# Moving the first six heads' convolutions into six PSUM banks, and four other steps within their queues, in a long-convolution attention and mixture-of-experts kernel

## The chip, the cores and the metric

One core of a Trainium2 chip. The metric is the device time of one launch in microseconds, here the median of three runs. The profile is one further execution, taken by the hardware profiler. TensorE is called PE, VectorE DVE, ScalarE ACT, GpSimd POOL and SyncE SP below.

## The reference, cut to what matters

The inputs x and ctx are 8 x 256 x 512 (batch, rows, positions). Rows form 32 heads of 8. With y the causal convolution of a head's 64 products of context rows with that head's 512 taps, the first block is

```python
kv = einsum('bhil,bhjl->bijhl', k_, v_)              # k = v = ctx
y = irfft(rfft(kv, n=2 * L) * rfft(ssm_kernel, n=2 * L))[..., :L]
out = einsum('bijhl,bhil->bjhl', y + kv * D, q_)     # q = layernorm(x)
x = x + out
```

and the second adds to x a feed-forward block of its layer norm: 16 experts (top 4 of a softmax, capacity 256, width 352) and a shared one of width 704, silu(x @ gate) * (x @ up) @ down. All is float32.

## The kernel before, in words

**Tiling.** Four heads make a group g, so there are eight groups (NG = 8, GH = 4). A group has two tiles of 128 tokens. Positions lie on the partitions in four blocks (LB = 4). A convolution is a product with Toeplitz matrices made of the taps: block row lb takes lb + 1 products, 10 in all. The products of context rows (pairs, i <= j only, 288 columns) are the moving operand. For heads 0 to 3 taps and pairs go in unsplit (line 510, 20 matmul records: each such product shows as two). From head 4 on both are split into a high and a low part, and three products are summed (line 517, 30 matmuls). The results go to the four PSUM banks of yb; two banks gu serve the feed-forward block, two banks mb the transposes.

**A head.** POOL makes the pairs (pairs, line 1081); ACT rounds them (round_kv, L832); POOL makes the low part (low_kv, L1092); PE convolves (convolve, L487 on). DVE multiplies by q in fifteen instructions (multiply, L1286; L1299 and L1301), or in thirty by halves, for heads 0 to 3: banks 0 and 1 as soon as they are done, then banks 2 and 3. Then it adds up (add_up, L1315), which counts d_sum. PE may begin the next head's bank pair when the multiplication of it is through (d_half for the first pair, d_mul for both).

**A group.** Each engine has a function steps(g, ...), and all order is the order of its queue and the semaphore waits in it. In steps(1) of PE: head 4; mixed_out(0), eight transposes of the four heads' sums into mb, which waits for four sums; head 5; normalised(0), transposes of the normalised tokens; prep_ctx(2), transposes of group 2's context; gate_up(0, 0) and (0, 1), products of the tokens with the shared weights (L580); head 6; gate_up 2 and 3 with the router; prep_q(2); head 7; gate_up 4 and 5. On DVE: multiply head 4, add_x(0) (adds x, then the token statistics), add up head 4, low_tokens(0), and so on by heads with the middle steps between, and prep_stats (statistics of x for the next group, L1265 to L1271) in head 1 of a group. POOL's inverse_t and inverse_x follow the statistics, ACT's norm_tokens and norm_q follow these.

**Weight pieces.** The shared weights come in seven pieces: 0 to 3 of gate and up, 4 to 6 of down. SP loads a piece, ACT rounds it (split_shared, L786), POOL (pieces 0, 1, 3; L1103) or DVE (2, 4, 5, 6; L1248) makes the low part. Raw pieces share room, so SP loads piece 3 when 0 is through, 5 when 2 is, 6 when 4 is (load_split_slot). Piece 2 lies where x1, the sum of add_x, comes to lie.

**SP's queue** around the change, in order: group 0's tiles; taps of heads 0 and 1; tiles of group 1; piece 0; taps of heads 2 and 3; pieces 1 and 2; when piece 0 is through, piece 3; when head 2 is convolved, the taps of head 4; tiles of group 2; then as below (lines 407 to 421).

```python
            sp.wait_ge(conv, 4)
            load_toep(5, 1)
            load_shared(LB)

            sp.wait_ge(conv, 5)
            load_toep(6, 0)
            sp.wait_ge(sw_h, 3)
            low_done(sp, 2)
            load_shared(LB + 1)
            load_split_slot(LB + 2)
            sp.wait_ge(conv, 6)
            load_toep(7, 1)
```

## Time and profile before

| | |
|---|---|
| median of three runs | 641.11 us (640.76 to 641.79) |
| the profiled execution: time, span | 641.18 us, 639.4 us |
| mean granted PE clock | 0.984 |
| PE busy | 597.3 us, 93% |
| DVE busy | 475.8 us, 74% |
| POOL busy | 352.6 us, 55% |
| ACT busy | 278.7 us, 44% |

The span runs from the first to the last instruction; 1.8 us of the execution lie around it. Times in a timeline are microseconds from the span's start. The granted clock is a share of 2.4 GHz. "Idle before" is the time for which an engine had nothing to do just before an instruction, with what ended it. POOL's spans are rough. The convolutions of heads 0 to 7 and the feed-forward steps of group 0 fill the first 94 us; groups 1 to 7 follow, then the experts.

### The profile page before, as it was taken

The page shows a single profiled execution, that of the slowest core. Times are in us where ns is not written, and L with a number is a line of the kernel's source. Part 1 is how long each engine was busy: PE and PEld are TensorE (multiplying, and loading weights), DVE is VectorE, ACT ScalarE, POOL GpSimd, SP SyncE. Part 2 cuts the span into 40 slices and gives each one's busy share as a digit, 9 for nine tenths or more (in the row PEclk, how much of TensorE's full clock was granted, in tenths as well). Part 3 has the DMA queues.
Part 4 walks back from the last instruction along what each step waited for, and adds up shares of the span by engine and source line. Part 5 has one row for each costly group of instructions (what it writes and reads, how often), then busy time and mean ns, then how long its engine had stood idle before and what let it go on. Part 6 is the DMA issues. An engine that isn't in the chain of part 4 may idle for free.

```text
span 639.4 us, 13527 instructions
## 1 busy us (share of the span) xinstructions
PE 597.3 (93%) x4447; PEld 560.3 (88%) x4447; DVE 475.8 (74%) x1226; ACT 278.7 (44%) x499; POOL 352.6 (55%) x481
## 2 busy tenths in 40 slices
PE   4976999999999999999999989899999999999993
PEld 3666989999999999999999878889999999999992
DVE  4998877848768677777589868898878877888630
ACT  2341442423423423424342243466556656655731
POOL 6946787866857666676662363226534344333342
PEclk9987989999999999999999999999999999999997
DMA  7471513414225115222040051968888877888543
GB/s 191 160 210 67 197 34 100 132 37 142 89 67 164 54 53 156 66 82 82 33 118 17 26 176 38 322 172 263 231 258 226 227 208 229 233 237 238 152 55 44
DMA packets 49882, 89.27 MB, mean 140 GB/s; under 512 B 3924, under 2 KB 20308, under 8 KB 49832
## 3 DMA queue, kind: packets, MB, share of 16 engines
q1 hardware_dynamic: 42560, 71.77, 35.5%
q0 software_dynamic: 7168, 16.78, 12.5%
q8 instruction: 28, 0.46, 0.3%
q14 instruction: 22, 0.18, 0.1%
q10 hardware_dynamic: 104, 0.08, 0.1%
HBM read 71.66 MB, written 16.95 MB: 139 GB/s over the span
## 4 chain that ended last, share of the span: by engine, by line
PE 80%; DVE 9%; DMA 3%; issue 3%; POOL 2%; ACT 1%; DVEq 1%; POOLq 0%; ACTq 0%; SPq 0%
PE gu L580 17%; PE yb L517 16%; PE gu L716 13%; PE mb L731 10%; PE gu L610 7%; PE yb L716 7%; PE mb L484 3%; PE yb L510 2%; PE yb L484 2%; DVE prod L1299 1%; DVE prod L1301 1%; DMA raw_w<-in_L_ffn_w_up_dram 1%; PE yb L690 1%; DMA xg<-normalised_tokens,slot_rows 1%; DVE onehot L1542 1%
## 5 line engine op out<-in xcount | busy, mean ns | idle before, releaser
L580 PE MATMUL gu<-xT,sw 128*128 128x256 f32 (+2 forms) x1152 | 141.6, 281 | 0.0
L580 PEld LDWEIGHTS gu<-xT,sw 128*128 128x128 f32 (+2 forms) x1152 | 137.4, 180 | 0.3
L517 PE MATMUL yb<-kvh,toep 128*128 128x288 f32 x560 | 120.9, 304 | 6.0 <-DVE prod L1301 6.0
L1299 DVE TENSOR_TENSOR prod<-yb,qT 128x96 f32<-128x96 f32 (+11 forms) x288 | 78.5, 283 | 42.9 <-PE yb L517 37.6
L1092 POOL TENSOR_TENSOR kvl<-kv,kvh 128x1152 fp32r<-128x1152 f32 x28 | 75.2, 2686 | 55.9 <-ACT kvh L832 55.7
L1081 POOL TENSOR_TENSOR kv<-kT 128x256 f32 (+3 forms) x232 | 104.7, 492 | 0.0
L517 PEld LDWEIGHTS yb<-kvh,toep 128*128 128x128 f32 x560 | 94.7, 194 | 6.6 <-issue 6.6
L517 PE MATMUL yb<-kvl,toep 128*128 128x288 f32 x280 | 84.5, 302 | 0.0
L1315 DVE TENSOR_REDUCE oT<-prod 128x256 f32<-128x2048 f32 x32 | 72.9, 2278 | 0.1
L1301 DVE TENSOR_TENSOR prod<-yb,qT 128x96 f32<-128x96 f32 (+10 forms) x252 | 67.4, 267 | 0.0
L832 ACT ACTIVATE kvh<-kv 128x1152 fp32r<-128x1152 f32 x28 | 32.7, 1168 | 76.5 <-PE yb L517 42.4
L731 PE MATMUL mb<-ed,midh 128*128 128x512 f32 x180 | 57.5, 400 | 0.0
L1565 DVE TENSOR_TENSOR ew<-raw_w,ew 128x704 fp32r<-128x704 f32 x64 | 55.0, 882 | 0.8 <-ACT ew L952 0.8
L517 PEld LDWEIGHTS yb<-kvl,toep 128*128 128x128 f32 x280 | 54.6, 195 | 0.0
L1100 POOL TENSOR_TENSOR midl<-mid,midh 128x256 fp32r<-128x256 f32 x38 | 28.5, 758 | 41.1 <-ACT midh L848 41.1
L610 PE MATMUL gu<-sd,midh 128*128 128x512 f32 x160 | 49.8, 393 | 0.2 <-DVE midl L1359 0.2
L1200 POOL MEMSET carrier<- 128x1 f32 x16 | 2.1, 129 | 84.3 <-DVE slot_rows L1559 84.3
L716 PE MATMUL gu<-xgT,ew 128*128 128x256 f32 x384 | 47.2, 282 | 0.6 <-issue 0.6
L952 ACT ACTIVATE ew<-raw_w 128x704 fp32r<-128x704 f32 x64 | 45.4, 778 | 4.6 <-DMA raw_w<-in_L_ffn_w_up_dram 4.6
L716 PEld LDWEIGHTS gu<-xgT,ew 128*128 128x128 f32 x384 | 46.4, 189 | 0.9 <-issue 0.8
L716 PE MATMUL gu<-xT,ew 128*128 128x256 f32 x384 | 47.0, 282 | 0.0
L716 PEld LDWEIGHTS gu<-xT,ew 128*128 128x128 f32 x384 | 46.3, 190 | 0.2 <-issue 0.2
(182 smaller groups left out, 1073.0 us busy)
## 6 DMA issues: line engine op xcount, KB each, us to landing
toep<-toeplitz_taps SPq DMA_DIRECT2D x28, 512.0 KB, 3.6
raw_w<-in_L_ffn_w_gate_dram SPq DMA_DIRECT2D x16, 704.0 KB
raw_w<-in_L_ffn_w_up_dram SPq DMA_DIRECT2D x16, 704.0 KB
raw_d<-in_L_ffn_w_down_dram SPq DMA_DIRECT2D x16, 512.0 KB, 4.3
c_t<-in_ctx_dram SPq DMA_DIRECT2D x16, 256.0 KB, 4.5
x_t<-in_x_dram SPq DMA_DIRECT2D x16, 256.0 KB, 4.8
normalised_tokens<-xn SPq DMA_DIRECT2D x16, 256.0 KB, 2.9
out_dram<-yo SPq DMA_DIRECT2D x16, 256.0 KB, 3.0
```

What stands on the lines that cost most here:

```text
L517: last = pe.matmul(yb[:, lb, 0:PW], toep[s][:, a, d:d + P], rhs[:, s, m, :], start=(i == 0), stop=(i == len(steps) - 1))
L580: last = pe.matmul(gu[0:m, i % 2, u * GT:(u + 1) * GT], sw[:, c, a, col:col + m], xT[:, c, b, :], start=(c == 0 and (a, b) == PASSES[0]), ...
L610: last = pe.matmul(gu[:, t, :], (midh, midl)[a][:, j, cols], sd[:, j, b, :], start=False, stop=(j == SJ - 2 and (a, b) == PASSES[-1]))
L716: last = pe.matmul(egu[j][0:m, u * CAP:(u + 1) * CAP], ew[k][:, c, a, col:col + m], xgT[k][:, c, b, :], start=(c == 0 and (a, b) == PASSES ...
L731: last = pe.matmul(mb[:, h, :], lhs[0:EK[j], EJ * k + j, h * P:(h + 1) * P], ed[k][0:EK[j], j, b, :], start=(j == 0 and (a, b) == PASSES[0 ...
L952: act.activation(ew[k][:, c, 0, :], raw_w[k][:, c, :], ACT.Copy).then_inc(ew_h, 1)
L1081: last = pool.tensor_tensor(to[:, :, POFF[d]:POFF[d] + w], src[:, :, 0:w], src[:, :, d * B:HD * B], ALU.mult)
L1092: pool.tensor_tensor(kvl[:, s, :, :], kv[:, s, :, :], kvh[:, s, :, :].bitcast(fp32), ALU.subtract)\
L1299: last = dve.tensor_tensor(prod[:, s, lo:hi, d * B // 2:HD * B // 2, d, :], pair, first, ALU.mult)
L1301: last = dve.tensor_tensor(prod[:, s, lo:hi, 0:w // 2, HD - d, :], pair, second, ALU.mult)
L1315: dve.tensor_reduce(oT[:, :, hl * HD * B:(hl + 1) * HD * B].rearrange("p c (a u) -> p c a u", u=2), prod[:, s, :, :, :, :].rearrange("p c ...
L1565: dve.tensor_tensor(ew[k][:, c, 1, :], raw_w[k][:, c, :], ew[k][:, c, 0, :].bitcast(fp32), ALU.subtract).then_inc(ew_l, 1)
```

## The change

Heads 1, 2, 4 and 5 get other homes: half a head is a pair of banks, and the six banks of yb and gu are handed round among them; free() holds what each half has to wait for. Heads 4 and 5 are multiplied by halves, head 3 is not any more, and head 4's second half is multiplied first, after the whole convolution. mixed_out(0) and normalised(0) go between the halves of heads 4 and 5, on DVE add_x(0) goes ahead of head 4's multiplication and low_tokens(0) behind it. The statistics of x of group 1 go from head 1 of group 0 to ahead of head 0, their inverse on POOL ahead of head 5's pairs, and SP loads that x before the context. Weight piece 2 goes from DVE to POOL, ahead of piece 1. On DVE pieces 4 and 5 go one head later: 4 from behind head 4 to behind the x statistics in head 5, 5 from there to head 6. On ACT head 5's rounding and the evacuation of q go ahead of piece 3. SP's queue is otherwise as before.

```diff
--- before.py
+++ after.py
@@ -285,7 +285,7 @@
         carried = [sem("carried0"), sem("carried1")]
         N_CONST = 9
         SW_PIECES = LB + SJ // 2
-        POOL_PIECES = (0, 1, 3)
+        POOL_PIECES = (0, 2, 1, 3)
         DVE_PIECES = [p for p in range(SW_PIECES) if p not in POOL_PIECES]
 
         def low_done(eng, piece):
@@ -307,8 +307,16 @@
                 return kv[:, n, :, :]
             return kv_more[n - 2][:]
 
+        BY_HALVES = (0, 1, 2, GH, GH + 1)
+
         def by_halves(n):
-            return isinstance(n, int) and n < GH
+            return isinstance(n, int) and n in BY_HALVES
+
+        FIRST_HOMES = {1: ((gu, 0), (yb, 0)), 2: ((yb, 2), (gu, 0)), GH: ((gu, 0), (yb, 0)),
+                       GH + 1: ((yb, 2), (yb, 0))}
+
+        def home(n, half):
+            return FIRST_HOMES.get(n, ((yb, 0), (yb, 2)))[half] if isinstance(n, int) else ((yb, 0), (yb, 2))[half]
 
         ROUND = [slice(0, TT * (NG - 2)), slice(TT * (NG - 2), NT)]
 
@@ -387,9 +395,10 @@
             load_first(1)
             sp.wait_ge(taps_hl, 1)
             sp.dma_start(toep_dram, padhl[:].bitcast(fp32)).then_inc(taps_out, 16)
+            sp.wait_ge(x_stat, 1)
+            load_group(1, parts="x")
             sp.wait_ge(c_tr, TT)
-            sp.wait_ge(x_stat, 1)
-            load_group(1)
+            load_group(1, parts="c")
             load_shared(0)
             load_first(2)
             load_first(3)
@@ -484,6 +493,21 @@
                     last = pe.transpose(dst[:, c * P:(c + 1) * P], src(c), ident[:])
                 return last
 
+            def free(n, half):
+                if isinstance(n, int) and n < GH + 2:
+                    if n == 1 and half == 1:
+                        pe.wait_ge(d_half, 1)
+                    if n == 2:
+                        pe.wait_ge(*((d_mul, 1), (d_half, 2))[half])
+                    if n == 3:
+                        pe.wait_ge(*((d_mul, 2), (d_half, 3))[half])
+                    if n == GH:
+                        pe.wait_ge(d_mul, (3, 4)[half])
+                    if n == GH + 1:
+                        pe.wait_ge(*((d_mul, 4), (d_half, 4))[half])
+                elif half == 0:
+                    wait(pe, d_mul, n)
+
             def convolve(n, hl, between=None):
                 s = hl % 2
                 if whole(n):
@@ -497,24 +521,27 @@
                     pe.wait_ge(kv_l, n + 1 - GH)
                     pe.wait_ge(toep_in[s], 16 * ((n - GH - s) // 2 + 1) if isinstance(n, int)
                                else n * 8 - (8 * GH - 16 + 8 * s))
-                wait(pe, d_half if by_halves(n) else d_mul, n)
+                free(n, 0)
                 for lb in range(LB):
-                    if by_halves(n) and lb == LB // 2:
-                        last.then_inc(conv_half, 1)
+                    if lb == LB // 2:
+                        if by_halves(n):
+                            last.then_inc(conv_half, 1)
                         if between:
-                            between(0)
-                        wait(pe, d_mul, n)
+                            between()
+                        free(n, 1)
+                    bank, at = home(n, lb // 2)
+                    at += lb % 2
                     if whole(n):
                         for m in range(lb + 1):
                             d = (LB - 1 - lb + m) * P
-                            last = pe.matmul(yb[:, lb, 0:PW], toep[s][:, n // 2, d:d + P].bitcast(fp32),
+                            last = pe.matmul(bank[:, at, 0:PW], toep[s][:, n // 2, d:d + P].bitcast(fp32),
                                              whole_kv(n)[:, m, :], start=(m == 0), stop=(m == lb))
                         continue
                     steps = [(m, a, b) for m in range(lb + 1) for a, b in PASSES]
                     for i, (m, a, b) in enumerate(steps):
                         d = (LB - 1 - lb + m) * P
                         rhs = (kvh, kvl)[b]
-                        last = pe.matmul(yb[:, lb, 0:PW], toep[s][:, a, d:d + P], rhs[:, s, m, :],
+                        last = pe.matmul(bank[:, at, 0:PW], toep[s][:, a, d:d + P], rhs[:, s, m, :],
                                          start=(i == 0), stop=(i == len(steps) - 1))
                 last.then_inc(conv, 1)
 
@@ -562,8 +589,8 @@
                 j = ORDER[i]
                 if isinstance(g, int) and g == 0 and i == 0:
                     pe.wait_ge(sw_h, LB)
-                    low_done(pe, 2)
                     low_done(pe, 3)
+                    pe.wait_ge(d_mul, GH + 1)
                 pe.wait_ge(n_h, TT * g + TT)
                 pe.wait_ge(n_l, TT * g + TT)
                 if i < TT:
@@ -613,16 +640,15 @@
                         last.then_inc(dn_mm, 1)
 
             def steps(g, prep, post, chunk):
-                convolve(GH * g, 0)
-                if post:
+                if chunk:
+                    convolve(GH * g, 0)
                     mixed_out(g - 1, g)
-                if chunk:
                     down(g - 2)
-                if post and chunk:
                     normalised(g - 1)
-                convolve(GH * g + 1, 1)
-                if post and not chunk:
-                    normalised(g - 1)
+                    convolve(GH * g + 1, 1)
+                else:
+                    convolve(GH * g, 0, lambda: mixed_out(g - 1, g))
+                    convolve(GH * g + 1, 1, lambda: normalised(g - 1))
                 if prep:
                     prep_ctx(g + 1)
                 if post:
@@ -643,7 +669,7 @@
 
             pe.wait_ge(consts, 2)
             prep_ctx(0)
-            convolve(0, 0, prep_q)
+            convolve(0, 0, lambda: prep_q(0))
             prep_ctx(1)
             convolve(1, 1)
             pe.wait_ge(gate_in, 16)
@@ -931,9 +957,9 @@
             split_shared(2)
             norm_q(1)
             round_kv(GH, 0)
+            round_kv(GH + 1, 1)
+            evacuate(qT, 1, q_tr, q_ev, d_mul, 0)
             split_shared(3)
-            evacuate(qT, 1, q_tr, q_ev, d_mul, 0)
-            round_kv(GH + 1, 1)
             steps(1, True, True, (4, 5, None, 6))
             steps(2, True, True)
             with act.Fori(3, NG - 1) as g:
@@ -1147,10 +1173,11 @@
             pairs(2, 0, 2)
             pairs(3, 0, 3)
             pairs(GH, 1, 0)
+            inverse_x(1)
             pairs(GH + 1, 1, 1)
             split_shared(0)
-            inverse_x(1)
             low_kv(GH, 0)
+            split_shared(2)
             low_kv(GH + 1, 1)
             split_shared(1)
             steps(1, True, True, False)
@@ -1285,15 +1312,18 @@
 
             def multiply(n, g, hl):
                 s = hl % 2
-                dve.wait_ge(conv_half if by_halves(n) else conv, n + 1)
+                if by_halves(n) and n != GH:
+                    dve.wait_ge(conv_half, BY_HALVES.index(n) + 1)
+                else:
+                    dve.wait_ge(conv, n + 1)
                 dve.wait_ge(q_ev, TT * g + TT)
                 wait(dve, d_sum, n - 1)
                 q = qT[:, bass.ds(g % 2, 1), :, hl * HD * B:(hl + 1) * HD * B].rearrange("p s c w -> p (s c) w")
 
-                def blocks(lo, hi):
+                def blocks(lo, hi, bank=yb, at=0):
                     for d in range(HD):
                         w = (HD - d) * B
-                        pair = yb[:, lo:hi, POFF[d]:POFF[d] + w].rearrange("p c (a u) -> p c a u", u=2)
+                        pair = bank[:, at:at + hi - lo, POFF[d]:POFF[d] + w].rearrange("p c (a u) -> p c a u", u=2)
                         first = q[:, lo:hi, 0:w].rearrange("p c (a u) -> p c a u", u=2)
                         second = q[:, lo:hi, d * B:HD * B].rearrange("p c (a u) -> p c a u", u=2)
                         last = dve.tensor_tensor(prod[:, s, lo:hi, d * B // 2:HD * B // 2, d, :], pair, first, ALU.mult)
@@ -1301,10 +1331,13 @@
                             last = dve.tensor_tensor(prod[:, s, lo:hi, 0:w // 2, HD - d, :], pair, second, ALU.mult)
                     return last
 
-                if by_halves(n):
-                    blocks(0, LB // 2).then_inc(d_half, 1)
+                if by_halves(n) and n == GH:
+                    blocks(LB // 2, LB, *home(n, 1)).then_inc(d_half, 1)
+                    blocks(0, LB // 2, *home(n, 0)).then_inc(d_mul, 1)
+                elif by_halves(n):
+                    blocks(0, LB // 2, *home(n, 0)).then_inc(d_half, 1)
                     dve.wait_ge(conv, n + 1)
-                    blocks(LB // 2, LB).then_inc(d_mul, 1)
+                    blocks(LB // 2, LB, *home(n, 1)).then_inc(d_mul, 1)
                 else:
                     blocks(0, LB).then_inc(d_mul, 1)
 
@@ -1457,15 +1490,16 @@
                     add_x(g - 1)
                 if not prep:
                     start_round_one()
+                if post and not chunk:
+                    add_x(g - 1)
                 multiply(GH * g, g, 0)
                 if post and not chunk:
-                    add_x(g - 1)
+                    low_tokens(g - 1)
                 if chunk:
                     chunk_sum(g - 2, [0])
                 add_up(GH * g, g, 0)
                 if chunk:
                     chunk_sum(g - 2, [1])
-                if post:
                     low_tokens(g - 1)
                 for piece in extra[0:1]:
                     if piece:
@@ -1475,7 +1509,7 @@
                     if post:
                         middle(g - 1, 2 * hl - 2)
                     add_up(GH * g + hl, g, hl)
-                    if isinstance(g, int) and g == 0 and hl == 2:
+                    if isinstance(g, int) and g == 0 and hl == 1:
                         dve.wait_ge(gate_h, 1)
                         dve.tensor_tensor(sw[:, :, 1, IS:UP], mb[:, 0, 0:LB * E].rearrange("p (c e) -> p c e", c=LB),
                                           sw[:, :, 0, IS:UP].bitcast(fp32), ALU.subtract).then_inc(gate_l, 1)
@@ -1483,7 +1517,7 @@
                         low_rest(g - 1)
                     if post:
                         middle(g - 1, 2 * hl - 1)
-                    if prep and hl == 1:
+                    if prep and post and hl == 1:
                         prep_stats(g + 1)
                     for piece in extra[hl:hl + 1]:
                         if piece:
@@ -1521,9 +1555,9 @@
             link(dve.tensor_tensor(before_in_b[:], same_b[:], later_row[:], ALU.mult))
             dve.wait_ge(first_out, 16)
             dve.wait_ge(taps_out, 16)
+            prep_stats(1)
             steps(0, True, False, False)
-            split_shared(2)
-            steps(1, True, True, False, (4, 5, None, 6))
+            steps(1, True, True, False, (None, 4, 5, 6))
             steps(2, True, True, True)
             with dve.Fori(3, NG - 1) as g:
                 steps(g, True, True, True)
```

## Rows read from the trace of the kernel before

**Rows 1.** The page, busy time of each engine.

```profile
PE 597.3 (93%) x4447; PEld 560.3 (88%) x4447; DVE 475.8 (74%) x1226; ACT 278.7 (44%) x499; POOL 352.6 (55%) x481
```

**Rows 2.** Table of windows: busy us (x instructions) by engine, clock, DMA share, GB/s.

```profile
52.80:59.60 6.80, 6.80 (x31) 6.80 (x32) 5.07 (x10) 1.52 (x2) 3.56 (x4) 0.55 0.01 3
...
94.00:350.00 256.00, 256.00 (x1906) 246.53 (x1905) 190.14 (x547) 91.67 (x160) 168.94 (x250) 1.00 0.29 87
```

**Rows 3.** Timeline of PE: start, us, instruction, idle before.

```profile
43.42 0.37 PE L517 MATMUL yb<-kvh,toep 128*128 128x288 f32 x1 [1.44 <-DVE prod L1301]
...
52.80 0.58 PE L517 MATMUL yb<-kvh,toep 128*128 128x288 f32 x1 [4.31 <-DVE prod L1301]
...
63.05 5.87 PE L580 MATMUL gu<-xT,sw 128*80 128x256 f32 x48
...
82.43 0.37 PE L517 MATMUL yb<-kvh,toep 128*128 128x288 f32 x1 [0.25 <-DVE prod L1301]
...
88.01 5.80 PE L580 MATMUL gu<-xT,sw 128*128 128x256 f32 x48
```

**Rows 4.** Timeline of DVE, 16 to 80 us.

```profile
16.37 0.47 DVE L1299 TENSOR_TENSOR prod<-yb,qT 128x128 f32<-128x128 f32 x2 [3.16 <-ACT qT L824]
...
18.99 0.47 DVE L1299 TENSOR_TENSOR prod<-yb,qT 128x128 f32<-128x128 f32 x2 [0.49 <-PE yb L510]
...
29.75 0.14 DVE L1283 COPY carrier_d<-carrier_d 128x1 f32<-128x1 f32 x1
...
32.06 0.46 DVE L1299 TENSOR_TENSOR prod<-yb,qT 128x128 f32<-128x128 f32 x2
...
41.14 0.47 DVE L1299 TENSOR_TENSOR prod<-yb,qT 128x128 f32<-128x128 f32 x2 [0.44 <-PE yb L510]
...
45.51 4.04 DVE L1252 TENSOR_TENSOR sw<-x,sw 128x704 fp32r<-128x704 f32 x2
...
49.48 0.71 DVE L1299 TENSOR_TENSOR prod<-yb,qT 128x256 f32<-128x256 f32 x2
...
52.58 1.28 DVE L1325 TENSOR_TENSOR x<-mb,x_t 128x512 f32<-128x512 f32 x2
...
74.73 2.62 DVE L1270 TENSOR_SCALAR xnm<-xmv 128x2 f32<-128x2 f32 x1
...
77.33 1.84 DVE L1259 TENSOR_TENSOR sd<-x,sd 128x512 fp32r<-128x512 f32 x2
```

**Rows 5.** Timeline of SP's DMA queue.

```profile
9.80 1.20 SPq L330 DMA_DIRECT2D c_t<-in_ctx_dram  x2
...
33.03 0.39 SPq L340 DMA_DIRECT2D toep<-toeplitz_taps  x1
...
63.95 1.12 SPq L355 DMA_DIRECT2D yo<-in_L_ffn_sw_down_dram  x2
...
65.75 0.59 SPq L340 DMA_DIRECT2D toep<-toeplitz_taps  x1
```

**Rows 6.** DMA issues at 11, 33 and 65.8 us: size, us to landing.

```profile
x_t<-in_x_dram SPq DMA_DIRECT2D x2, 256.0 KB, 5.2
...
toep<-toeplitz_taps SPq DMA_DIRECT2D x1, 512.0 KB, 7.6
...
toep<-toeplitz_taps SPq DMA_DIRECT2D x1, 512.0 KB, 5.5
```

**Rows 7.** Timeline of POOL, 28 to 78 us.

```profile
28.73 3.33 POOL L1106 TENSOR_TENSOR sw<-sw_raw,sw 128x704 fp32r<-128x704 f32 x2
...
32.23 0.69 POOL L1059 TENSOR_TENSOR xrs<-xve,half_neg 128x2 f32<-128x2 f32 x1 [0.17 <-DVE xve L1271]
...
46.45 4.64 POOL L1106 TENSOR_TENSOR sw<-sw_raw,sw 128x704 fp32r<-128x704 f32 x2
...
74.66 2.67 POOL L1092 TENSOR_TENSOR kvl<-kv,kvh 128x1152 fp32r<-128x1152 f32 x1 [2.54 <-ACT kvh L832]
```

**Rows 8.** Timeline of ACT, group 0's first silu.

```profile
69.15 0.38 ACT L838 ACTIVATE sil<-gu 64x256 f32<-64x256 f32 x1
```

## The prediction

> **What bounds the kernel now.** I read the page first: TensorE (PE) is busy for 597.3 of 639.4 us [rows 1]. Next the table of windows: from 94 to 350 us PE has no idle time, at a full clock [rows 2], so the later stage neither waits for what is changed nor hides it. A microsecond by which PE reaches its work at 88 us earlier comes off the end. What matters lies before that, and PE's timeline gives the fixed points: head 4 begins at 43.42, head 5 at 52.80 behind 4.31 us of idle time, gate_up of group 0 at 63.05, head 7 at 82.43, and gate_up goes on at 88.01 [rows 3]. The waits ahead of heads 4, 5 and 7 were ended by VectorE (DVE), whose own timeline, read third, is nearly closed from 19 to 58 us. The windows show what an idle PE costs beside the gap: behind the 4.31 us the granted clock was 0.55 over 6.80 us, that is mostly the lower of its two levels, 1.2 GHz [rows 2]. The timeline of the DMA queue comes last; it decides here.
>
> I measure against the profiled execution, 641.18 us (span 639.4 and 1.8 around it); the median of the three runs is 641.11, the same thing. About 0.2%, 1.3 us, is what a measurement of this kernel can tell from no change.
>
> **Second x statistics.** They hold DVE from 29.75 to 32.06, 2.3 us in the middle of its closed stretch. Their new place is ahead of head 0's multiplication, where DVE is idle for 3.16 us before 16.37 [rows 4]. SP issues the two x tiles first, from 9.80, where the context tiles were [rows 5]; landing took 5.2 us [rows 6], so the second is there at 15.6, the statistics end near 17.5 and the multiplication starts 1.1 late. Of this 0.49 is taken up by the idle time before its second half at 18.99 [rows 4]. Net: about 1.8 us gained. The context tiles go out 1.2 later and land before 17; PE reads them behind head 0, after 18: nothing.
>
> **Heads 0 to 3 in six banks.** With heads 1 and 2 partly in gu, PE runs ahead of DVE and has head 3 done near 36, so DVE takes that in one piece. One piece costs 3.1 us (49.48 to 52.58); a half costs 2.1 (16.37 to 18.99 less the idle 0.49), two 4.2; and the 0.44 us of idle time inside head 3 goes [rows 4]: 1.6 us. Together the four sums, before at 45.51, are ready near 42. The gate's rounding, 0.2 us, only changes its place.
>
> **Weight piece 2.** It leaves DVE, where it stood between heads 3 and 4 for 4.04 us [rows 4], and comes to POOL, where such a piece takes 3.33 [rows 7]. POOL's queue is then: pairs of head 4, x inverse (0.69 us and a small product, 0.9), pairs of head 5, piece 0, low part of head 4, piece 2, low part of head 5, piece 1. With 2.67 for a low part it is empty near 45; with 4.64 for each of the last two pieces [rows 7] at 47.5; the token inverse behind it is wanted at 47.7. So: nothing, but with a cover of 0.2 to 3 us. The page GPSIMD Engine Reference of the Trainium skill (Engine selection) calls two-input elementwise work about twice as slow there and gives it to VectorE. The trace disagrees for this place: 3.33 us on POOL, 4.04 on DVE. By that rule POOL's piece would be 8 us and the inverse some 2 to 5 us late.
>
> **First mixed rows inside head 4.** SP's queue sets the date. POOL's piece 0 ends 0.9 later (the x inverse is ahead of it), so the taps of head 4, issued at 33.03 [rows 5] and landed 7.6 us later [rows 6], are there at 41.5. Before, PE wanted them at 43.42; now it has been idle since 37. Head 5, behind 4.31 us of idle time, took 6.7 us for 30 products, at about 0.24 each in its slow part [rows 2, 3]; I take the same for head 4. The first 9 products end at 43.7, the eight transposes at 45.1, the other 21 near 49. DVE's x addition, which now stands ahead of head 4's multiplication, starts at 44.4 where it had 52.58 [rows 4]; 3.2 us later its statistics are out, POOL's inverse ends at 48.6, ACT's first normalised tile at 49.4. Head 5's first half starts at 49.0 in its own banks, the transposes follow at 50.3, the second half ends at 54.1. DVE multiplies head 4 by halves, 49.0 to 53.1, and does the low tokens to 54.4. So the context transposes come then and gate_up begins at 55.3 instead of 63.05: **7.7 us** ahead. Its new wait for head 4's multiplication was met at 53.1.
>
> **Group 1 up to head 7.** DVE: sum of head 4 to 56.6, head 5 by halves to 60.7 (1.1 dearer than whole, but piece 4's 1.8 is gone from ahead of it). POOL: token inverse, piece 3, pairs of head 6 until near 55.6; ACT's first silu, bound to these, came at 69.15 [rows 8] and comes at 60.2. Both meet at 61, for DVE's first middle step. From there I keep the old spacing: the scalar step of the statistics, 74.73, comes at 65.8, **8.9 us** ahead. Then comes piece 4, where piece 5 was; that ended at 79.1 [rows 4], piece 4 ends at 70.2.
>
> **What is late next.** SP waits for piece 4's low part before it issues piece 6, and behind that in its queue stands the load of head 7's taps. Before, piece 4 was done ahead of head 5's multiplication: piece 6 was issued at 63.95, the taps at 65.75 [rows 5], 5.5 us to landing [rows 6], 11 us before head 7 wanted them. Piece 4 now stands behind head 5, two middle steps and the statistics. Done at 70.2, it lets the taps go at 72.1; they land at 77.6. DVE frees the yb banks 3.2 us after piece 4, at 73.4, and PE is ready then. Head 7 waits 4.1 us for its taps and begins at 77.6 instead of 82.43: only **4.8 us** ahead. PE stands still for over 4 us again, so I price head 7 like head 5, 6.7 us instead of 5.6 [rows 3], and gate_up follows at 84.3 instead of 88.01: **3.8 us**. Piece 6, the store and the next tiles shift with SP; head 8's taps go out near 76.5 and land by 84, before head 8 at 90. DVE's piece 5 fits ahead of head 7's end.
>
> **The sum.** gate_up gains 7.7; DVE adds 1.2; the taps take back 4.1; the clock 1.0: 3.8 us, all passed on by the closed PE stage. 641.2 less 3.8 is 637.4. Bounds: landings of 512 KB taps are 5.5 and 7.6 us [rows 6], so the stall can be 2 us longer (gain 1.7); head 4 at full clock would bring DVE's chain 1 us forward (gain 4.8).
>
> **Rivals.** (1) The taps stall, but less. The small scalar step in the x statistics took 2.62 us at 74.73 [rows 4], 0.07 us behind the start of POOL's 2.67 us low part at 74.66 [rows 7]. If POOL gets there a little later, that step is through first, and piece 4 and the taps come 2.4 us sooner; with head 4 at full clock too, 3.4. The gain is 6.2 to 7.2: 634 to 635. The page SBUF — State Buffer of the Trainium skill (Who interferes with whom) has a lock on a shared port pair, held by whoever issues first; the lengths, 2.62 beside 2.67, agree. For it: POOL has more work ahead. Against: both follow the same middle step, so the order may well repeat. Chance 0.22.
> (2) No stall: head 7 at 73.5, 8.7 us ahead, 632.5. It needs the taps within 1.3 us of issue, or another order in SP's queue, which the diff doesn't make. Chance 0.06, for an error in my reading of the queue.
> (3) About nothing: landings of 7.6 us, a slow clock for longer, and the cover at POOL's inverse gone by 1 us leave under 1.3. Chance 0.09.
> (4) **Slower,** by the same SP wait. Head 7 starts 7.4 us after piece 4 ends; it breaks even if piece 4 ends at 75.0 instead of 70.2, and each microsecond beyond costs one. It decides if POOL's token inverse is 7 us later than my sum, as with piece 2 at 8 us and its neighbours at 4.64. With 2 more the time is 643. No row here has a piece that long. Chance 0.04.
> The case of the sum has 0.59, its own range 635.4 to 639.4.
>
> **The numbers.** Faster by over 0.2%: 0.59, 0.22 and 0.06, 0.87. Same 0.09, slower 0.04. For eight in ten the range takes in rival (1) and the longer stall: 633.4 to 639.6.
>
> **What would show it.** The four sums near 42; the x addition near 44; gate_up at 55 to 56; the taps of head 7 issued 1.9 us behind DVE's piece 4; PE's wait before head 7 put down to that transfer, 3 to 6 us, with a low clock behind it; no new idle time of PE after 94. Wrong if head 7 starts as soon as head 6 is multiplied, if head 4 doesn't wait for its taps, or if POOL's inverse of tokens comes late.

## The result, and the profile after

The changed kernel takes 636.88 us (median of four runs, 634.94 to 637.20) beside 641.04 us before (four runs); the ratio is 0.9934, 95% interval 0.9923 to 0.9946. That is 4.2 us faster, forecast were 3.8 us and 637.4. The same kernel was run again later (636.51 us) and profiled a second time; where the two profiles of it differ, both are given below, since what differs between them can't be read as the effect of an edit.

The page of the changed kernel, its span and busy times, beside [rows 1]:

```profile
span 634.8 us, 13541 instructions
...
PE 596.0 (94%) x4447; PEld 559.9 (88%) x4447; DVE 474.2 (75%) x1239; ACT 278.9 (44%) x499; POOL 348.3 (55%) x483
```

PE does the same 4447 matmuls in almost the same busy time (596.0 us, before 597.3), in a span that is 4.6 us shorter: 3.3 us of what went is idle time, 1.3 us is busy time. The timeline of PE, for [rows 3]:

```profile
41.82 0.58 PE L544 MATMUL gu<-kvh,toep 128*128 128x288 f32 x1 [3.44 <-DMA toep<-toeplitz_taps]
...
44.12 1.50 PE L493 MATMUL mb<-ident,oT 128*128 128x128 f32 x8
...
55.32 5.83 PE L607 MATMUL gu<-xT,sw 128*80 128x256 f32 x48
...
77.95 0.58 PE L544 MATMUL yb<-kvh,toep 128*128 128x288 f32 x1 [3.93 <-DMA toep<-toeplitz_taps]
...
84.11 5.82 PE L607 MATMUL gu<-xT,sw 128*128 128x256 f32 x48
```

The mixed rows stand inside head 4, gate_up of group 0 begins at 55.32 instead of 63.05, 7.7 us ahead. Head 7 begins only 4.5 us ahead, at 77.95, and it is a transfer that it waited for, for 3.93 us. gate_up goes on at 84.11 instead of 88.01: 3.9 us. In the second profile of the same kernel everything here is 0.6 to 1.9 us earlier:

```profile
41.20 0.37 PE L544 MATMUL gu<-kvh,toep 128*128 128x288 f32 x1 [3.65 <-DMA toep<-toeplitz_taps]
...
76.61 0.58 PE L544 MATMUL yb<-kvh,toep 128*128 128x288 f32 x1 [3.64 <-DMA toep<-toeplitz_taps]
...
82.24 5.80 PE L607 MATMUL gu<-xT,sw 128*128 128x256 f32 x48
```

The two waits for taps are there in both, the rest of this section is the first profile. The table of windows, for [rows 2], shows (us, busy time and instructions of each engine, granted clock, DMA share, GB/s) the low clock behind each gap and the stage behind it:

```profile
41.00:44.00 3.00, 2.18 (x9) 2.21 (x10) 2.53 (x4) 0.00 (x0) 3.00 (x3) 0.61 1.05 253
...
46.00:50.00 4.00, 3.59 (x28) 3.35 (x26) 3.81 (x18) 1.48 (x3) 1.24 (x3) 1.00 0.20 57
...
78.00:84.00 6.00, 6.00 (x30) 6.00 (x31) 2.23 (x2) 0.40 (x1) 6.00 (x11) 0.61 0.91 270
...
94.00:350.00 256.00, 256.00 (x1907) 246.54 (x1905) 189.05 (x547) 91.38 (x159) 165.62 (x246) 1.00 0.29 87
```

The clock is 0.61 over 41 to 44 us, behind the gap before head 4, and 0.61 behind that before head 7; from 94 to 350 us PE is as closed as before. DVE's timeline, for [rows 4]:

```profile
15.00 0.15 DVE L1310 COPY carrier_d<-carrier_d 128x1 f32<-128x1 f32 x1 [1.77 <-DMA x_t<-in_x_dram]
...
20.78 0.47 DVE L1329 TENSOR_TENSOR prod<-yb,qT 128x128 f32<-128x128 f32 x2 [1.10 <-PE yb L537]
...
41.28 2.29 DVE L1348 TENSOR_REDUCE oT<-prod 128x256 f32<-128x2048 f32 x1
...
45.28 1.29 DVE L1358 TENSOR_TENSOR x<-mb,x_t 128x512 f32<-128x512 f32 x2 [1.72 <-PE mb L493]
...
66.58 2.62 DVE L1297 TENSOR_SCALAR xnm<-xmv 128x2 f32<-128x2 f32 x1
...
69.19 1.83 DVE L1286 TENSOR_TENSOR sd<-yo,sd 128x512 fp32r<-128x512 f32 x2
```

The statistics run in the idle stretch at 15.00, the last of the four sums is at 41.28 to 43.5, the x addition at 45.28 instead of 52.58. The scalar step still takes 2.62 us, and piece 4 comes behind it, at 69.19. The DMA queue, for [rows 5], then the landing of the taps of head 7, for [rows 6]:

```profile
34.60 0.39 SPq L348 DMA_DIRECT2D toep<-toeplitz_taps  x1
...
71.09 0.88 SPq L363 DMA_DIRECT2D yo<-in_L_ffn_sw_down_dram  x2
...
72.66 0.59 SPq L348 DMA_DIRECT2D toep<-toeplitz_taps  x1
```

```profile
toep<-toeplitz_taps SPq DMA_DIRECT2D x1, 512.0 KB, 5.0
```

DVE's piece 4 ends at 71.02, SP issues piece 6 at 71.09 and the taps at 72.66. They land 5.0 us later, at 77.7. Head 7 starts 0.3 us behind that. This is the chain that the prediction gave, from end to end.

### The profile page after: what moved, and what is told of

The parts are those of the page before. It is cut to its first block, busy times and chain, and to the rows that moved or that the text cites. A ratio compares the mean times of both kernels' runs of the same rounds, so it can differ in the third digit from the quotient of the medians.

```text
span 634.8 us, 13541 instructions
## 1 busy us (share of the span) xinstructions
PE 596.0 (94%) x4447; PEld 559.9 (88%) x4447; DVE 474.2 (75%) x1239; ACT 278.9 (44%) x499; POOL 348.3 (55%) x483
## 4 chain that ended last, share of the span: by engine, by line
PE 79%; POOL 6%; DVE 5%; DMA 4%; issue 3%; ACT 1%; SPq 0%; POOLq 0%; DVEq 0%; ACTq 0%
PE gu L607 17%; PE yb L544 16%; PE gu L742 13%; PE mb L757 10%; PE gu L637 8%; PE yb L742 7%; PE mb L493 3%; PE yb L493 2%; POOL kv L1107 2%; DMA toep<-toeplitz_taps 2%; DMA xg<-normalised_tokens,slot_rows 1%; POOL kv_more L1107 1%; POOL sw L1132 1%; PE yb L716 1%; DVE onehot L1576 1%
## 5 line engine op out<-in xcount | busy, mean ns | idle before, releaser
L544 PE MATMUL yb<-kvh,toep 128*128 128x288 f32 x554 | 117.8, 300 | 3.9 <-DMA toep<-toeplitz_taps 3.9
L1329 DVE TENSOR_TENSOR prod<-yb,qT 128x64 f32<-128x64 f32 (+10 forms) x272 | 74.6, 285 | 41.0 <-PE yb L544 38.7
L544 PEld LDWEIGHTS yb<-kvh,toep 128*128 128x128 f32 x554 | 92.1, 191 | 4.1 <-issue 4.1
L544 PE MATMUL yb<-kvl,toep 128*128 128x288 f32 x277 | 82.7, 299 | 0.0
L1331 DVE TENSOR_TENSOR prod<-yb,qT 128x96 f32<-128x96 f32 (+10 forms) x238 | 64.1, 269 | 0.0
L544 PEld LDWEIGHTS yb<-kvl,toep 128*128 128x128 f32 x277 | 53.1, 192 | 0.0
```

The costliest lines, as they stand in the source:

```text
L544: last = pe.matmul(bank[:, at, 0:PW], toep[s][:, a, d:d + P], rhs[:, s, m, :], start=(i == 0), stop=(i == len(steps) - 1))
L1329: last = dve.tensor_tensor(prod[:, s, lo:hi, d * B // 2:HD * B // 2, d, :], pair, first, ALU.mult)
L1331: last = dve.tensor_tensor(prod[:, s, lo:hi, 0:w // 2, HD - d, :], pair, second, ALU.mult)
```

## The experiments

Times are medians; each run is measured beside the kernel before on the same chip, and "beside before" is its median less that one's. "Second gate_up" is where gate_up goes on behind head 7 in the profiled execution, "rest" its span less that. The ratio with its interval is the recorded estimate and not always the quotient of the two medians: for the change, again, the medians differ by 4.2 us, the ratio 0.9948 makes it 3.3.

| run | us | before there | beside before | ratio, 95% interval | second gate_up | rest |
|---|---|---|---|---|---|---|
| the change | 636.88 | 641.04 | -4.2 | 0.9934, 0.9923 to 0.9946 | 84.11 | 550.7 |
| the change, again | 636.51 | 640.66 | -4.2 | 0.9948, 0.9932 to 0.9964 | 82.24 | 550.9 |
| taps of head 7 first | 632.75 | 640.73 | -8.0 | 0.9874, 0.9860 to 0.9888 | 78.44 | 552.8 |
| piece 4 early | 633.62 | 640.73 | -7.1 | 0.9887, 0.9873 to 0.9901 | 78.07 | 554.9 |
| before, taps of head 7 first | 640.77 | 640.73 | 0.0 | 0.9999, 0.9990 to 1.0008 | 87.85 | 551.3 |
| taps of head 4 first | 636.22 | 640.73 | -4.5 | 0.9931, 0.9919 to 0.9943 | 85.49 | 550.9 |
| x statistics back | 637.48 | 640.22 | -2.7 | 0.9958, 0.9944 to 0.9972 | 85.39 | 550.7 |
| piece 2 back | 636.11 | 640.22 | -4.1 | 0.9940, 0.9927 to 0.9954 | 82.07 | 550.9 |
| POOL later | 635.43 | 640.22 | -4.8 | 0.9925, 0.9911 to 0.9939 | 82.96 | 550.7 |
| PE kept busy | 635.57 | 640.22 | -4.7 | 0.9931, 0.9917 to 0.9944 | 82.23 | 550.9 |
| mixed rows back | 643.36 | 640.66 | +2.7 | 1.0040, 1.0024 to 1.0055 | 89.23 | 551.0 |
| banks back | 637.14 | 640.66 | -3.5 | 0.9953, 0.9940 to 0.9965 | 83.73 | 550.8 |
| combined | 635.12 | 640.66 | -5.5 | 0.9907, 0.9885 to 0.9929 | 80.76 | 552.0 |

The last column bears out the base of the sum: with the second gate_up anywhere between 82.07 and 89.23, what follows takes 550.7 to 551.0 us in the profiles of this kernel, so a microsecond won there is one won at the end. Only where it lies under 81 do some get lost again. One profile is not enough to read an edit worth under 2 us: in the two of the change the second gate_up stands at 84.11 and 82.24, and its ten executions lie between 634.93 and 639.27 us.

**Is it SP's queue that holds head 7?** One edit to the changed kernel, and the same edit to the kernel before:

```diff
-            load_split_slot(LB + 2)
             sp.wait_ge(conv, 6)
             load_toep(7, 1)
+            load_split_slot(LB + 2)
```

> The changed kernel, with SP issuing the taps of head 7 ahead of its wait for weight piece 4; nothing else. My theory (head 7 waits for its taps behind that wait, and the clock falls in the gap): taps issued near 55, head 7 starts at 74.2 as soon as head 6 is multiplied, instead of 77.95, takes 5.6 instead of 6.2 us; 4.3 us off the changed kernel, about 632.5. Rival, that the wait only happens to stand there and POOL's low part or the transposes of q hold head 7 anyway: no change, 636.9.

> The kernel before, with the same order in SP's queue as in the run with head 7's taps first. My theory: before, those taps landed 11 us early, so nothing moves, 641.0 within 0.6. Rival, that the order in SP's queue by itself gains (other transfers sooner): 638 or less.

Measured 632.75 and 640.77. SP's and PE's timelines of the changed kernel with the taps first:

```profile
54.82 0.38 SPq L348 DMA_DIRECT2D toep<-toeplitz_taps  x1
...
74.39 0.37 PE L544 MATMUL yb<-kvh,toep 128*128 128x288 f32 x1 [0.24 <-DVE prod L1331]
...
78.44 5.80 PE L607 MATMUL gu<-xT,sw 128*128 128x256 f32 x48
```

The taps go out at 54.82, head 7 starts at 74.39, released by DVE's multiplication of head 6, and takes 4.05 us with a granted clock of 1.00, less than the 5.6 that I had allowed. The stall is gone; in the kernel before the same edit moves nothing. So the change made this wait, and some 3.8 us of its gain went into it. The second gate_up comes 5.7 us ahead of the changed kernel's first profile, yet its span is only 3.6 us shorter (3.8 and 1.9 beside the second). PE's list of waits behind it has a new row:

```profile
PE gu L626 <- POOL midl L1126: 1.2, 1, 1.2
```

The down projection of group 0 waits for POOL's last low part, which ran from 89.28 to 90.54 beside DVE's piece 6 at 88.67. That is 1.2 of the 2.1 us by which the rest grew; the other 0.9 is not traced to one wait.

**Or piece 4's place?** The other way to free SP:

```diff
-            steps(1, True, True, False, (None, 4, 5, 6))
+            steps(1, True, True, False, (4, None, 5, 6))
```

> The changed kernel, with piece 4 on DVE put back behind head 4's sum, where it stood before; pieces 5 and 6 as in the change. My theory: SP is let go near 58, the stall is gone; DVE is idle for 1.27 us ahead of its first middle step at 61.4, so 1.8 us of piece cost only 0.6 there: head 7 at 74.8, 3.7 us off, about 633.2. Rival (DVE bounds group 1, piece 4 there costs its whole 1.8 us): 634.4. Rival (the wait is not the cause): 636.9 or more.

Measured 633.62. The taps of head 7 go out at 59.74. The piece takes 1.33 us of DVE at 56.76, and the first middle step comes 0.7 us later than in the changed kernel's first profile (62.09, there 61.42). This run has the earliest second gate_up, 78.07, and the longest rest, 554.9: behind the same wait of 1.2 us for POOL the clock was 0.72 over 90 to 96 us, with head 7's taps first it was 1.00:

```profile
90.00:96.00 6.00, 5.13 (x16) 4.09 (x17) 5.82 (x20) 1.86 (x3) 5.56 (x12) 0.72 0.13 42
...
90.00:96.00 6.00, 5.20 (x23) 4.36 (x24) 5.82 (x20) 1.92 (x3) 5.57 (x12) 1.00 0.15 55
```

Both ways agree: the cause is piece 4's new place together with the order behind it in SP's queue.

**The taps of head 4.**

```diff
-            sp.wait_ge(sw_h, 1)
-            low_done(sp, 0)
-            load_shared(3)
             sp.wait_ge(conv, 3)
             sp.wait_ge(taps_out, 16)
             load_toep(4, 0)
+            sp.wait_ge(sw_h, 1)
+            low_done(sp, 0)
+            load_shared(3)
```

> The changed kernel, with SP issuing the taps of head 4 ahead of piece 3 (behind head 2's convolution, near 32, instead of 34.60). My theory: they land near 37.5 instead of 41.8, head 4's first half runs at full clock near 38.4, the mixed rows wait for the four sums at 43.5 instead of 44.1, DVE's x addition starts about 0.9 earlier, head 7's taps too: 636.0. Rival: the gap moves behind the first half and the clock falls there all the same, no change, 636.9. Other rival (the stall at head 4 costs what PE stood still, 3.4 us): 633.5.

Measured 636.22. PE and DVE of this run:

```profile
42.77 1.09 PE L493 MATMUL mb<-ident,oT 128*128 128x128 f32 x8 [4.04 <-DVE oT L1348]
...
43.54 1.29 DVE L1358 TENSOR_TENSOR x<-mb,x_t 128x512 f32<-128x512 f32 x2 [0.82 <-PE mb L493]
...
70.98 0.59 SPq L348 DMA_DIRECT2D toep<-toeplitz_taps  x1
...
78.69 0.58 PE L544 MATMUL yb<-kvh,toep 128*128 128x288 f32 x1 [6.34 <-DMA toep<-toeplitz_taps]
```

The first half of head 4 no longer waits; the transposes wait 4.04 us for the four sums. The x addition starts at 43.54, 1.7 us ahead of the first profile of the change (45.28) but 0.5 ahead of the second (44.02), and the taps of head 7 go out 1.7 and 0.6 us sooner. In this execution they took 7.5 us to land instead of 5.0 and 4.8, and all was lost again. The median's gain of 0.3 beside the change is within the intervals, so my theory and the rival without a gain can't be told apart; 633.5, the rival that prices all that PE stood idle, is out. What stands: the wait at head 4 was worth 0.5 to 1.7 us of the 3.4 us at the x addition, and the landing of 512 KB scatters by more.

**The second x statistics, undone.** prep_stats(1) back into head 1 of DVE's queue, the context tiles first on SP, inverse_x(1) behind piece 0 on POOL.

```diff
-            prep_stats(1)
             steps(0, True, False, False)
...
-                    if prep and post and hl == 1:
+                    if prep and hl == 1:
...
-            inverse_x(1)
             pairs(GH + 1, 1, 1)
             split_shared(0)
+            inverse_x(1)
```

> The changed kernel, with the second x statistics undone: they stand again in head 1 of DVE's queue, SP loads the context tiles before x, POOL's x inverse is again behind piece 0. In the changed profile DVE is idle for 1.10 us in head 0 and 1.72 us before the x addition. My theory: the sums come 2.3 us later, 45.8, of which the wait of 1.7 us before the x addition covers a part: the taps of head 4 (0.9 us sooner again) no longer bind, and the addition is 1 to 1.5 us later: 638.0. Rival, worth its full 2.3 us: 639.2. Rival, hidden altogether: 636.9.

Measured 637.48, 2.7 us under the kernel before where the change is 4.2 under it: 1.4 us for this part by the medians, 1.5 or 0.6 by the ratios of the change's two sets, whose intervals this one's overlaps. The covered case is the nearest of the three, but nothing is clear of the noise. The x addition starts at 46.04, where the two profiles of the change have 45.28 and 44.02.

**Piece 2 back on DVE.**

```diff
-        POOL_PIECES = (0, 2, 1, 3)
+        POOL_PIECES = (0, 1, 3)
...
             steps(0, True, False, False)
+            split_shared(2)
             steps(1, True, True, False, (None, 4, 5, 6))
```

> The changed kernel, with piece 2 on DVE again, between head 3's sum and the x addition. DVE is idle there for 1.72 us in the changed profile. My theory: the piece runs beside POOL's piece 1 and takes about 4 us, 43.5 to 47.5, so the addition is 2.3 us later: 639.2. Rival (POOL, lighter by one piece, is done with piece 1 sooner, DVE's piece takes 2 us): no loss, 637.2.

Measured 636.11: nothing lost, the rival was right. DVE's piece, and POOL's last one before it:

```profile
42.34 1.68 DVE L1279 TENSOR_TENSOR sw<-x,sw 128x704 fp32r<-128x704 f32 x2
...
44.09 1.48 DVE L1358 TENSOR_TENSOR x<-mb,x_t 128x512 f32<-128x512 f32 x2
...
39.09 3.34 POOL L1133 TENSOR_TENSOR sw<-sw_raw,sw 128x704 fp32r<-128x704 f32 x2
```

POOL is through with piece 1 at 42.43, so the same two instructions that took 4.04 us before take 1.68 and fill the idle stretch ahead of the x addition at 44.09. The 4.04 us [rows 4] were DVE's piece beside POOL's low part and piece, not the price of the work. With the other engine out of the way such a piece takes 1.68 us on DVE; POOL's took 3.34. The medians show nothing that moving piece 2 to POOL earned once the rest was changed.

**Rival (1): the held scalar step.** One wait more on POOL:

```diff
                 pool.wait_ge(kv_m, n)
+                if isinstance(n, int) and n == GH + 3:
+                    pool.wait_ge(x_stat, 3)
```

> The changed kernel, with one wait added on POOL: the low part of head 7 begins only when DVE's x statistics of group 2 are through. Rival (1) of the prediction by itself. If the scalar step of 2.62 us at 66.58 is held by POOL's instruction: it takes 0.2, the statistics end 2.4 us sooner, piece 4 (then beside POOL's low part) ends 1 to 2.4 sooner and the taps with it: 634.6 to 636. If the 2.62 us are the step's own: no gain, 636.9 or up to 2 more, since POOL is late.

Measured 635.43. DVE and POOL of this run, where the changed kernel had 66.58 and 69.19:

```profile
66.67 0.17 DVE L1299 TENSOR_SCALAR xnm<-xmv 128x2 f32<-128x2 f32 x1
...
66.81 3.75 DVE L1288 TENSOR_TENSOR sd<-yo,sd 128x512 fp32r<-128x512 f32 x2
...
67.08 2.94 POOL L1120 TENSOR_TENSOR kvl<-kv,kvh 128x1152 fp32r<-128x1152 f32 x1 [3.03 <-DVE xve L1300]
```

The scalar step takes 0.17 us instead of 2.62. So the 2.6 us were a wait for POOL's instruction: the Trainium skill's page SBUF — State Buffer (Who interferes with whom) has this lock, and trace and page agree. But piece 4 then runs beside the low part and takes 3.75 us instead of 1.83; it ends at 70.56, in the profiles of the change at 71.02 and 69.95. Its end lies 0.54 us behind that of POOL's low part (67.08 and 2.94), as if its second instruction had waited for that one. The time is handed on, not won, and the rival's 2.4 us were wrongly priced. Beside the kernel before it stands 0.6 us better than the change, not more than the intervals allow.

**The clock behind the gap.** 28 products into a bank that head 7 overwrites, while PE waits for the taps:

```diff
+                    if isinstance(n, int) and n == GH + 3:
+                        pe.wait_ge(d_mul, n)
+                        for _ in range(28):
+                            pe.matmul(yb[:, 3, 0:GT], sw[:, 0, 0, 0:P], xT[:, 0, 0, :], start=True, stop=True)
                     pe.wait_ge(kv_h, n + 1 - GH)
```

> The changed kernel, with 28 further products of 256 columns on PE while it waits for head 7's taps, behind the multiplication of head 6, into a bank that head 7 overwrites; the computation is as before. They take 3.4 us at full clock and end near 77.6, ahead of the taps at 77.9. My theory (the low clock behind the gap costs what I summed): head 7 takes 4.1 to 4.3 instead of 6.2 us, gate_up starts at 82.1 instead of 84.1, 634.9. Rival (the clock falls all the same, as PE was idle at 71 to 73 too, and the added work is in the way): 637 to 639.

Measured 635.57. PE of this run:

```profile
73.64 3.62 PE L523 MATMUL yb<-xT,sw 128*128 128x256 f32 x28 [0.15 <-DVE prod L1335]
...
78.18 0.37 PE L548 MATMUL yb<-kvh,toep 128*128 128x288 f32 x1 [0.92 <-POOL kvl L1122]
...
82.23 5.80 PE L611 MATMUL gu<-xT,sw 128*128 128x256 f32 x48
```

The wait of 0.92 us is put down to POOL's low part, but head 7's was done at 68.64; it is the taps, issued at 72.13 and landed 5.8 us later, at 77.9. The granted clock is 1.00 throughout, from 72.4 to 82.23. Head 7 takes 4.05 us, as where its taps went first; in the two profiles of the change it took 6.16 (clock 0.62) and 5.63 (0.69). So the low clock cost 1.6 to 2.1 us there. The whole kernel doesn't show it: the second gate_up at 82.23 is 1.9 us ahead of the change's first profile and level with its second (82.24), where the taps had landed 1.5 us sooner. The median stands 4.7 us under the kernel before, the change's 4.2: no gain that can be told from none.

**The mixed rows, undone.** Banks, pieces and statistics as in the change, the old order on PE and DVE:

```diff
-                    convolve(GH * g, 0, lambda: mixed_out(g - 1, g))
-                    convolve(GH * g + 1, 1, lambda: normalised(g - 1))
+                    convolve(GH * g, 0)
+                    mixed_out(g - 1, g)
+                    convolve(GH * g + 1, 1)
+                    normalised(g - 1)
...
-                if post and not chunk:
-                    add_x(g - 1)
                 multiply(GH * g, g, 0)
                 if post and not chunk:
-                    low_tokens(g - 1)
+                    add_x(g - 1)
...
                 add_up(GH * g, g, 0)
+                if post and not chunk:
+                    low_tokens(g - 1)
```

> The changed kernel, with the mixed rows and the normalised tokens behind heads 4 and 5 again on PE, and on DVE the x addition behind head 4's multiplication; banks, statistics and pieces as in the change. My theory: the addition starts at 52 instead of 45.3, the whole chain to the normalised tokens is in a row again, gate_up begins near 60 instead of 55.3, piece 4 and the taps of head 7 are 3.5 to 5 us later: 640 to 641.5, so this part carries nearly the whole gain. Rival (the taps' stall absorbs it, as it hid DVE's work): under 638.

Measured 643.36, 2.7 us slower than the kernel before, 6.8 slower than the change and beyond the 641.5 that I had allowed.

```profile
51.35 1.28 DVE L1360 TENSOR_TENSOR x<-mb,x_t 128x512 f32<-128x512 f32 x2
...
56.93 1.97 PE L493 MATMUL mb<-ident,xn 128*128 128x128 f32 x8 [4.44 <-ACT xn L830]
...
61.95 6.43 PE L607 MATMUL gu<-xT,sw 128*80 128x256 f32 x48
...
83.64 0.56 PE L544 MATMUL yb<-kvh,toep 128*128 128x288 f32 x1 [3.30 <-DMA toep<-toeplitz_taps]
```

The x addition is at 51.35, PE is idle for 4.44 us before the normalised tokens and its clock is 0.50 behind it, gate_up begins at 61.95, near the old 63.05. With piece 4 still in its new place the stall at head 7 (3.30 us) comes on top. This part carries the whole gain: without it the other parts, with piece 4's late place among them, are a loss. What they would be with SP's order mended as well was not run.

**The banks of heads 0 to 3, undone.** The old homes and halves for these heads:

```diff
-        BY_HALVES = (0, 1, 2, GH, GH + 1)
+        BY_HALVES = (0, 1, 2, 3, GH, GH + 1)
...
-        FIRST_HOMES = {1: ((gu, 0), (yb, 0)), 2: ((yb, 2), (gu, 0)), GH: ((gu, 0), (yb, 0)),
+        FIRST_HOMES = {GH: ((gu, 0), (yb, 0)),
...
+                    if 1 <= n < GH:
+                        pe.wait_ge(*((d_half, n), (d_mul, n))[half])
```

> The changed kernel, with heads 0 to 3 in the four yb banks by halves as before (head 3 by halves too); heads 4 and 5 as in the change. My theory: DVE's sums come 1.6 us later (45.1), the transposes wait for them instead of for the taps of head 4, the x addition is at 46.3 instead of 45.3: 1 us slower than the changed kernel. Rival (the banks matter more, since PE gets behind DVE in heads 1 to 3): 2 us or more. Rival, nothing, since the taps of head 4 bind: 0.

Measured 637.14, 0.6 us over the change run beside it, within the intervals. From the start of the third sum to that of the fourth DVE takes 6.39 us in this run (35.14, 41.53) and 5.42 and 5.43 in the two profiles of the change: 1.0 us on DVE. The x addition, at 45.05, lies between those two (45.28 and 44.02), so neither the profiles nor the medians separate the 1 us of the first theory from none; 2 us is not seen.

**Combined.** The taps of heads 7 and 4 first, by the two edits of SP's queue above, and pieces 4 and 5 in their old places:

```diff
-            steps(1, True, True, False, (None, 4, 5, 6))
+            steps(1, True, True, False, (4, 5, None, 6))
```

> The changed kernel, with SP issuing the taps of head 7 ahead of its wait for piece 4, the taps of head 4 ahead of piece 3, and DVE's pieces 4 and 5 where they stood before (behind head 4 and behind the x statistics). Both stalls gone, and head 7's multiplication no longer behind piece 5, which held it by 2 us where only head 7's taps were moved. Expected: head 7 near 73.3, no new wait of PE at the down projection; 1.5 to 2.5 us under the run with head 7's taps first, 630.5 to 631.5. Rival (POOL's low parts bind by then): 632.7, as that run.

Measured 635.12 (631.20 to 636.11), 2.4 over the run with head 7's taps alone: my forecast was wrong, though one of the six executions took 631.20.

```profile
56.08 3.77 DVE L1286 TENSOR_TENSOR sd<-yo,sd 128x512 fp32r<-128x512 f32 x2
...
56.41 2.89 POOL L1118 TENSOR_TENSOR kvl<-kv,kvh 128x1152 fp32r<-128x1152 f32 x1 [1.28 <-ACT kvh L858]
...
64.07 0.37 PE L544 MATMUL yb<-kvh,toep 128*128 128x288 f32 x1 [3.31 <-DVE prod L1331]
```

Piece 4 begins at 56.08 and POOL's low part of head 6 at 56.41; side by side the piece takes 3.77 us. In the run with piece 4 early it began at 56.76, POOL's low part only at 58.22, and it took 1.33. DVE frees the banks that much later, and PE waits 3.31 us before head 6, in that run 0.73. That this is the whole loss was read from one profile; no run moved the low part to test it. The best kernel measured is the changed one with the taps of head 7 first, 632.75 us.

## Why the prediction was right

By its own steps, forecast beside the two profiles of the changed kernel:

| step | forecast | first | second |
|---|---|---|---|
| four sums ready | 42 | 43.5 | 42.7 |
| taps of head 4 landed, head 4 begins | 41.5 | 41.82 | 41.20 |
| x addition | 44.4 | 45.28 | 44.02 |
| gate_up | 55.3 | 55.32 | 54.48 |
| scalar step of the statistics | 65.8 | 66.58 | 65.52 |
| piece 4 done | 70.2 | 71.02 | 69.95 |
| taps of head 7 issued, landed | 72.1, 77.6 | 72.66, 77.7 | 71.59, 76.4 |
| head 7 begins | 77.6 | 77.95 | 76.61 |
| second gate_up | 84.3 | 84.11 | 82.24 |

Every step of the chain is there, in its order. That the median came within 0.5 us of the forecast is in part luck: single executions of this kernel spread over 4.3 us, and the second profile's gate_up is 2.1 us ahead of the forecast's.

**Second x statistics:** this term was too large. They start at 15.00 and head 0's multiplication 1.2 us late, as forecast (1.1), but the 0.49 us of idle time behind its first half didn't take it up: it grew to 1.10, since the first transposes on PE took 1.91 us and head 0's other half came at 16.60 where PE had 15.39 before. So head 0's sum starts 1.8 us later than before (22.94, before 21.15; 22.12 in the second profile) and not 0.6. The run with the statistics undone puts the worth of the part for the whole kernel at 0.6 to 1.5 us, within the noise; forecast 1.8 on DVE.

**Banks:** forecast 1.6 us on DVE. Beside the kernel before it is 1.6 (7.06 us from the third sum to the fourth, 5.42 after), beside the run without the part 1.0; at the end 0.6 by the medians, which can be none. PE's wait for the taps of head 4 can hide a part of DVE's gain, as the same sum had it.

**Piece 2:** the conclusion "nothing on POOL" holds (token inverse at 48.68, POOL idle for 3.26 us ahead of it). The gain of 4.04 us was mis-sized: the piece would have cost 1.68 us in the new order, in idle time. So was the comparison of 3.33 us on POOL with 4.04 on DVE, by which the prediction said that the trace disagreed with VectorE as the faster place: the 4.04 had been taken beside POOL's work, and with POOL idle it is 3.34 against 1.68, a factor of two. The total was not hurt, since the sum went by POOL's cover and the taps of head 4 and never by these 4 us alone.

**Mixed rows:** right in size (7.7 us at gate_up) and shown to carry the gain. Two errors cancelled in the first profile: the clock came back sooner than I took it (it was 0.96 over 45 to 46 us; the forecast's 49 for the end of head 4 puts it near 47), and the x addition was 0.9 us later.

**What is late next:** right, shown by undoing it from either end. **The clock:** 6.7 us forecast for head 7, 6.16 measured, so the term of 1.0 in the sum was 0.6, and nothing in the second profile, 5.63 (head 7 took 5.6 before, at a clock of 0.70). The whole price of the low clock there is larger, 1.6 to 2.1 us: it takes 4.05 with no gap ahead.

**Rivals:** (2) did not occur. Its 632.5 is what the kernel gives once the order in SP's queue is mended, 632.75. (1) fell: the lock is real, but its 2.4 us are handed to the next instruction; it was priced as if nothing stood behind the step. (3) fell with landings of 5.0 and 4.8 us. (4), slower, is not the change's case; taken without the mixed rows the other parts do come out slower than before, by 2.7 us, with the stall as one part.

Between the second gate_up (3.9 us) and the span (4.6 us) 0.7 us stay open: the rest is 551.4 us before and 550.7 after (550.9 in the change's second profile, 551.3 in the kernel before with head 7's taps first), and no experiment was made on it.

## What to carry to other kernels

When work is moved on one engine, look for queues on others that wait for it, and read what stands behind that wait: here a load with 11 us to spare became the bound because a piece of low parts ahead of it went one head later. A duration taken beside another engine's work isn't the price of an instruction (4.04 and 1.68 us for a piece of 128x704, 3.75, 1.83 and 1.33 for one of 128x512); before it is booked as a gain or moved, ask what runs beside it in the new place. And once one wait is gone, the gain holds only until the next engine is late: of 5.7 us at the second gate_up the mended order kept 3.6 in the span. And profile the changed kernel twice before one profile is compared with another: here two of the same kernel were 1.9 us apart at the point that mattered.

## What the runs showed of the hardware

A DVE piece of two 128x512 instructions from SBUF to SBUF took 3.75 and 3.77 us beside POOL's low part and 1.33 with POOL idle for all but 0.2 us of it (1.83 beside smaller POOL instructions); one of two 128x704 instructions took 4.04 us beside POOL's low part and piece and 1.68 with POOL idle; a scalar step of 0.17 us took 2.62 when it came 0.06 us behind the start of POOL's 2.66 us instruction. The landing of the 512 KB of head 7's taps, by the list of DMA issues, took from 4.4 us (mixed rows back) to 7.5 (taps of head 4 first) in ten executions of the changed kernel and its variants in which they were issued behind piece 6; 3.1 us of scatter are as much as most of the edits here are worth. Issued ahead of it they took 3.6, 3.6 and 3.5 us, and head 4's taps 3.3 and 3.4 us ahead of piece 3, 6.7 to 8.0 behind it: what was issued just ahead of a load seems to lengthen its landing too, though no run holds the time of issue fixed. And 28 products that serve nothing kept the granted clock at its upper level (1.00) over a gap: head 7 then took 4.05 us instead of 6.16 or 5.63, and the kernel's time didn't fall clear of the noise.
